# Identity products on TensorE ahead of the experts, and another order for the first expert's output

## The reference

```python
topk_idx = jax.lax.top_k(tmp, K)[1]                 # 8 experts of 64 for each of the 4096 tokens
...
buf = jnp.zeros((E, CAP + 1, h), x.dtype).at[e, pos_c].set(x[token])[:, :CAP]   # 256 slots per expert
g = jnp.einsum('ech,ehi->eci', buf, w_gate)
u = jnp.einsum('ech,ehi->eci', buf, w_up)
y = jnp.einsum('eci,eih->ech', jax.nn.silu(g) * u, w_down)
...
out = jnp.zeros((n, h), jnp.float32).at[token].add(y_slots * w_slot[:, None])
```

## Time and profile before

| | us |
|---|---|
| median of 3 runs | 990.7 (989.04 to 995.75) |
| the profiled execution, its time | 979.64 |
| the profiled execution, its span | 977.9 |
| PE busy in the span | 740.0 (76%) |
| DVE busy | 511.8 (52%) |
| POOL busy | 508.8 (52%) |
| PEld busy | 482.2 (49%) |
| ACT busy | 401.6 (41%) |
| mean granted TensorE clock | 0.874 of full speed |

### The profile page before, as it was taken

The page is one execution under the profiler, slowest core; times in us unless marked ns, Lnnn a source line. Parts: engine busy times, 40 slices in busy tenths (PEclk is TensorE's granted clock), DMA queues, the critical chain, the costliest instruction groups (busy, mean ns, idle before and its releaser), DMA issues.

```text
span 977.9 us, 15569 instructions
## 1 busy us (share of the span) xinstructions
PE 740.0 (76%) x4819; PEld 482.2 (49%) x4819; DVE 511.8 (52%) x2009; ACT 401.6 (41%) x884; POOL 508.8 (52%) x514
## 2 busy tenths in 40 slices
PE   5678999989988989989978974200999988888200
PEld 3344656546545555555554542200888776776100
DVE  3176568867777769768767664720222222222038
ACT  3237556654655646555633441100444343333100
POOL 5000001164466375464565655775488888887630
PEclk9879899997999989989978888555899999999555
DMA  8694877645646456455253659301899999898878
GB/s 304 183 331 150 287 290 234 213 161 185 212 160 226 169 173 203 136 176 175 96 179 92 194 150 279 100 26 42 237 277 284 268 213 165 155 168 184 209 220 327
DMA packets 165262, 191.47 MB, mean 196 GB/s; under 512 B 21753, under 2 KB 146709, under 8 KB 165180
## 3 DMA queue, kind: packets, MB, share of 16 engines
q1 hardware_dynamic: 128764, 134.14, 43.0%
q0 software_dynamic: 30720, 38.03, 19.0%
q10 hardware_dynamic: 5696, 18.30, 5.0%
HBM read 100.64 MB, written 110.67 MB: 216 GB/s over the span
## 4 chain that ended last, share of the span: by engine, by line
PE 37%; issue 16%; DVE 15%; DMA 12%; POOL 8%; ACT 4%; SPq 4%; another core or an unknown queue 3%; ACTq 1%; POOLq 0%; DVEq 0%
DMA acc_d<-ys,xg 9%; POOL acc_d L808 6%; PE outT L1147 5%; DVE junk L1425 4%; PE scores L1105 4%; PE scoresT L1127 4%; PE scoresT L1131 4%; PE stageA L1071 4%; PE scoresT L1368 3%; PE stageA L1087 3%; PE stageC L1206 1%; PE turns L1157 1%; PE stageC L1188 1%; SPq L525 1%
## 5 line engine op out<-in xcount | busy, mean ns | idle before, releaser
L730 POOL DMA_INDIRECT slots_d<-H,dest x256 | 258.2, 1009 | 199.7 <-issue 65.2
L1425 DVE CUSTOM_DVE_ANT_0 junk<-scores,mask 128x256 bf16<-128x256 f32 x512 | 188.6, 420 | 99.6 <-PE scores L1105 64.4
L808 POOL DMA_INDIRECT acc_d<-ys,xg x128 | 198.2, 1548 | 60.9 <-issue 29.6
L869 ACT ACTIVATE PT<-scoresT 128x512 f32<-128x512 f32 (+1 forms) x320 | 152.6, 511 | 70.5 <-PE scoresT L1131 52.9
L1368 PE MATMUL scoresT<-xgT,wgu 128*128 128x256 f32 x512 | 127.6, 393 | 23.5 <-ACT xgT L984 21.5
L1127 PE MATMUL scoresT<-mask,identb 128*128 128x512 bf16 (+1 forms) x320 | 114.4, 358 | 18.5 <-ACT PT L869 10.8
L1368 PEld LDWEIGHTS scoresT<-xgT,wgu 128*128 128x128 f32 x512 | 96.3, 194 | 48.2 <-ACT xgT L984 32.1
L1105 PE MATMUL scores<-Ks,Qs 96*128 96x256 bf16 x512 | 105.5, 290 | 12.6 <-DVE mrowmax L1425 9.4
L1131 PE MATMUL scoresT<-Qs,Ks 98*128 98x256 bf16 (+1 forms) x640 | 115.0, 263 | 0.0
L1147 PE MATMUL outT<-PT,Va 128*32 128x256 f32 (+1 forms) x1280 | 93.8, 365 | 0.0
L1131 PEld LDWEIGHTS scoresT<-Qs,Ks 98*128 98x128 bf16 x640 | 65.9, 103 | 41.4 <-issue 11.3
(11 more groups left out here) (267 smaller groups left out, 1139.8 us busy)
## 6 DMA issues: line engine op xcount, KB each, us to landing
xg<-slots_d SPq DMA_DIRECT2D x64, 324.0 KB
slots_d<-blank ACTq DMA_DIRECT2D x26, 648.0 KB, 4.6
parts_d<-parts SPq DMA_DIRECT2D x32, 384.0 KB, 3.0
Qs<-parts_d SPq DMA_DIRECT2D x96, 128.0 KB
Ks<-parts_d SPq DMA_DIRECT2D x90, 128.0 KB
acc_d<-zero SPq DMA_DIRECT2D x32, 272.0 KB
wgu<-L_ffn_w_gate_dram SPq DMA_DIRECT2D x64, 128.0 KB
wgu<-L_ffn_w_up_dram SPq DMA_DIRECT2D x64, 128.0 KB
```

The source lines that it names most:

```text
L730: pool.indirect_dma_start(out=slots_d[:, :], in_=H2[bt.par][:, t, :], in_offset=None, out_offset=bass.IndirectOffsetOnAxis(ap=dest[bt.par] ...
L808: pool.indirect_dma_start(out=acc_d[ACC[e]][:, :], in_=ys[e % NY][:, h, :], in_offset=None, out_offset=bass.IndirectOffsetOnAxis(ap=xg[e % ...
L869: sc_.activation(PT[m % NPT][:, :, 0:w], src, ACT.Exp).then_inc(sems["exp"], 1)
L1425: ins = v.tensor_tensor_reduce(out=junk[:, i, :], in0=bS[n % 2][:, i * 2 * P:(i + 1) * 2 * P], in1=mask[:, edge, :], scale=1.0, scalar=TAK ...
```

## The change

Four things are changed:

- The first 20 of the last batch's 32 sends count on a semaphore of their own, `s_most`. SP, ahead of the slots' loads, waits for that one too, and for 20 sends less on the semaphore of the odd batches, so for the same 256 sends in all.
- PE, behind `late_cnt`, waits for those 20 sends, then makes 76 products of the identity with itself (128 x 128, f32) into the bank `bO`. Nobody reads them.
- PE: `turn_x(0)`, `expert(0)`, `turn_x(1)`, `expert_out(0)`, and only then `expert(1)`; from there on as before.
- ACT runs `silu(0)`, `take_x(1)`, `scale_y(0)`, and then `silu(1)`; DVE runs `hidden(0)` ahead of `take_x(1)`.

```diff
+MOST = 20
...
+        s_most = sem("most_rows_of_last_batch_sent")
...
             store_x1(last)
+            sp.wait_ge(s_most, 16 * MOST)
             for i in range(2):
-                sp.wait_ge(sent[i], 16 * T * K * B // 2)
+                sp.wait_ge(sent[i], 16 * (T * K * B // 2 - (MOST if i == last.par else 0)))
...
-                    bounds_check=last_slot, oob_is_err=False).then_inc(sent[bt.par], 16)
+                    bounds_check=last_slot, oob_is_err=False
+                    ).then_inc(s_most if bt.b == B - 1 and i < MOST else sent[bt.par], 16)
...
             take_x(0)
-            for e in range(E):
+            silu(0)
+            take_x(1)
+            scale_y(0)
+            for e in range(1, E):
                 silu(e)
                 if e < E - 1:
                     take_x(e + 1)
-                if e > 0:
+                if e > 1:
                     scale_y(e - 1)
             scale_y(E - 1)
...
+            def idle_products(n):
+
+                for i in range(n):
+                    mm(bO[:, 0:P], ident[:], ident[:], start=True, stop=True)
+
+            pe.wait_ge(s_most, 16 * MOST)
+            idle_products(76)
             turn_x(0)
-            for e in range(E):
+            expert(0)
+            turn_x(1)
+            expert_out(0)
+            for e in range(1, E):
                 expert(e)
                 if e < E - 1:
                     turn_x(e + 1)
-                if e > 0:
+                if e > 1:
                     expert_out(e - 1)
             expert_out(E - 1)
...
             take_x(0)
-            for e in range(E):
+            hidden(0)
+            take_x(1)
+            for e in range(1, E):
                 if e < E - 1:
                     take_x(e + 1)
                 hidden(e)
```

## The result

The changed kernel takes 1004.0 us in the median of 9 runs (992.91 to 1011.41), the kernel before 990.7 in 9 (980.69 to 995.84). The ratio is 1.0158, with a 95% interval of 1.0112 to 1.0204: slower, where 2.5 us of gain were forecast. The profiled execution of the changed kernel is a long one, 1011.41 us, and already its last send comes at 698.27 instead of 677.96. So I count from the last send, as both kernels do the same up to there.

The account below looks back on a forecast made before the run. POOL's back-to-back scatters were taken as the bound; the third scatter moving from 698.86 to 696.4 gains 2.5 us, so 979.64 becomes 977.1 profiled, 988.2 against the median; range 979.5 to 993.5.

Parts of the forecast that it names:

- What bounds the kernel: Experts: POOL's scatters run back to back in 1.853 us steps, so the end is the run's start plus a constant.
- Part 1: PE before the experts: products start at 664.8, take 18.8 us and end at 683.6, delaying the first transposes 0.4 us.
- The price of one product: PE's identity products: 0.215 us each at the full clock, 0.43 at 1.2 GHz, as two instructions.
- The lower bound of that sum: Earliest end of the products, with 3.4 us cold and 0.215 us each: 682.7, so nothing is late.
- Part 2: First expert at the full clock: first scatter 6.9 us after its transposes, at 690.5, 4.6 us earlier.
- Part 3: Second expert in the new order: third scatter 12.8 us after the first transposes, at 696.4; gain 2.5 us.
- is worth nothing by itself: First two experts: the new order neither gains nor costs time where the products do their work.
- Rival 3: PE's products take twice as long, 32.7 us, from a cold clock or serial loads; 14.3 us late, about 1005; chance 0.04.

Follow-up runs that it names:

- h2_spaced: The changed kernel with each of the last 11 sends waiting for the landing of the one before; third scatter 20.1 us behind the last send.
- j1_shifted: The changed kernel with 20 more identity products at the start of PE's program, on a chip without the waits; one execution, 926.54 us.
- e1_order: The changed kernel without its 76 products, new order and split semaphore kept; ratio 1.0017 to the kernel before.
- h1_changed: The changed kernel itself measured once more, on a chip with the waits; ratio 1.0100 to the kernel before.
- f3_bf16: 240 products of the bf16 identity in place of the changed kernel's 76 in f32; third scatter 31.7 us behind the last send.

## Why the prediction was wrong, step by step

- **What bounds the kernel**: right. In every run the distance from the third scatter to the last is 237.0 to 238.0 us, whatever stands ahead. What is won or lost at the start of the experts reaches the end, a loss of 11.6 us as well.
- **Part 1, the 76 products**: this is the step that failed. The price of one product was right: 152 matmuls take 18.7 us in h2_spaced and 18.74 in j1_shifted, where 18.8 were forecast. (The lower bound of that sum comes to 682.8, not 682.7.) What was wrong is the sentence that they fill 18.4 us "in which PE now does nothing", as if an idle engine were free to use. On the chips with the waits, while POOL issues its sends back to back, PE gets some 86 instructions through (once 111) and then one per 0.7 to 1.4 us, until some 7 us behind the last send (once 3.8). So the stream took 718.46 - 685.05 = 33.4 us, and the transposes came 20.2 us behind the last send instead of 5.7.
- **The Trainium skill's rule** ("TensorE: Matmul & The Clock Gate", Part 3), by which a load of the same row groups would not overlap a matmul: the measurement decides against it, with 152 pairs of load and matmul in 18.7 us, the cold ones included.
- **Part 2**: right. The first scatter came 725.33 - 718.46 = 6.87 us behind the transposes; 6.9 were forecast.
- **Part 3**: right in its mechanism. The hole in front of the third scatter is 2.00 us, and the third scatter comes 12.34 us behind the transposes, where 12.8 were forecast. That the order "is worth nothing by itself" was off: 0.5 us, in two pairs of runs.
- **Rival 3**, the slower side, had the size (14.3 us to the transposes; they were 14.9 us late) and the wrong cause: the clock did rise at 691, and the loads were hidden. It got 0.04. A chance for "PE doesn't get its instructions at this rate beside the sends" was missing. The profile of before hinted at it, with DVE's wait of 3.7 us for itself beside the sends.
- **The remainder**: 11.6 us are 1.2%, the ratio's interval begins at 1.1% and its middle is 1.6%. The first stage of the profiled execution of the changed kernel is 20 us longer than that of before; e1_order, which has all edits but the products, shows no such loss (1.0017), and over the other runs the last send (where it isn't spaced) lies anywhere from 674.8 to 696.9 on chips with the waits. I put the 20 us down to this spread; no experiment was made on it.

**What stays open.** What PE is short of in the halt isn't in the profile: a semaphore isn't what it waits for, the DMA engines are nearly idle (share 0.02 to 0.04), and it ends only when the sends have. But it is not PE's alone. DVE's short instructions, further ahead in the changed kernel but also beside sends, come in such steps:

```profile
669.61 0.29 DVE L1544 TENSOR_TENSOR sc<-sc,wsum 128x128 f32<-128x128 f32 x1 [1.22 <-DVE wsum L1544]
671.01 0.23 DVE L1544 TENSOR_SCALAR H<-sc 128x128 f32<-128x128 f32 x1 [1.11 <-DVE sc L1544]
```

They are 1.40 us apart, and PE's steps in the halts are 0.70 or 1.40 (only h1_changed has others among them). Both engines even keep one beat: from DVE's `near` at 675.21 to PE's first held load at 694.10 it is 18.89 us, 27 times 0.70. In five of the other six traces with a halt these two starts also lie a multiple of 0.70 us apart, to within 0.03; h1_changed is the exception. This points at something that both engines share, and not at a limit of PE's own; what it is isn't shown.

Two rules of the Trainium skill come near. "Runtime: NRT & Kernel Launch" (Instruction fetch mechanics) says that an engine's instructions arrive in blocks of 256 by a DMA queue of the sequencer's own, mostly hidden. The profile's page of the changed kernel agrees with the blocks (40 packets, 0.66 MB, so 16 KB each):

```profile
q8 instruction: 40, 0.66, 0.3%
```

The number of packets also goes, roughly, with PE's instructions: 39 in the kernel before, 40 in the changed one with 304 more, 41 in f3_bf16 with 480 more. A late block would stop PE at a fixed place, and it would have to land where the halt ends. The traces have none there. In the changed kernel a packet of q8 starts at 688.5 and takes 1.3 us, so it is done before the halt begins at 693; the next starts at 727.4. Between 690 and 706 the queues moved (packets, MB, share):

```profile
q1 hardware_dynamic: 971, 1.19, 27.3%
q0 software_dynamic: 384, 0.04, 2.0%
q14 instruction: 1, 0.01, 0.1%
```

The one packet of q14 comes 5.4 us behind the last send; in the kernel before there is one 5.3 us behind it. In the other six traces with a halt q8 has no packet in it or at its end either. So a late block is not the cause. Whether a count of instructions or a place in PE's stream starts the halt stays open: h1_changed ran 25 instructions further than the changed kernel, which speaks for neither in a strict form, and j1_shifted, made to tell them apart, didn't meet the right chip.

"NOTIFIC — the notification-queue block" (7.1, on overflow) says that the block which writes an engine's records holds its producers back rather than lose one inside. A store of records that fills at some 86 instructions, and is emptied slowly while the sends go on, would look like this, and the beat that PE and DVE share would fit it; it would then be an effect of being profiled. No run here shows it, and none without a profile was there to compare.

## What to carry to other kernels

Filling an idle engine is not always free: ask what it shares with the engines that work, and whether the trace shows any engine waiting for its own last result in that stretch, for no work of others. That was the one sign ahead of time. Where TensorE is to be warmed, use few and long instructions and put them close to the work: here 14 matmuls of 512 columns gave the one measured gain, and 80 instructions or fewer beside dense indirect DMAs were not held. And read a change at the start of a serial run in one distance, from an event that both kernels share to the run's beginning; here it told the 0.5 us of the new order, where the interval of a total was 4 us wide to either side.

## What was not expected of the hardware

- On four chips of the experiments, and where the kernel before and the change were first measured, back to back indirect DMAs of POOL (steps of 1.28 us) hold PE to 85 to 111 instructions and then one per 0.7 to 1.4 us, and many of DVE's short dependent instructions start in steps of 0.70 us or a multiple of it. Steps of 2.4 us don't. On two chips nothing is held, and the kernel before takes 926 to 929 us there against 982 to 992.
- The halt costs the clock too: the windows above have it at 1.00 until 696 and at 0.50 from 699 on. From 708 to 710 it is 0.91, some 3 us after the stream had resumed at 705.3.
